# Half the key stores, and each head's 128 key rows as two loads of the same 64 rows

## The reference, cut to what matters

```python
x = _ln(src) * (1.0 + scale) + shift
q = (x @ Wq + bq).reshape(B, S, N_HEAD, HEAD_DIM).transpose(0, 2, 1, 3)
k = (x @ Wk + bk).reshape(B, S, N_HEAD, HEAD_DIM).transpose(0, 2, 1, 3)
v = (x @ Wv + bv).reshape(B, S, N_HEAD, HEAD_DIM).transpose(0, 2, 1, 3)
scores = jnp.einsum('bhqd,bhkd->bhqk', q / math.sqrt(HEAD_DIM), k)
scores = scores + attention_bias                     # 2 x 16 x 2048 x 2048 floats, 512 MB
scores = jnp.where(src_mask, -jnp.inf, scores.astype(jnp.float32))
probs = jax.nn.softmax(scores, axis=-1).astype(v.dtype)
ctx = jnp.einsum('bhqk,bhkd->bhqd', probs, v)
ctx = ctx.transpose(0, 2, 1, 3).reshape(B, S, D)
x = x + (ctx @ Wo + bo)
h = _ln(x) * g2 + beta2
ff = _gelu2(h @ W1 + b1) @ W2 + b2
return x + ff
```

## Time and profile before

| | |
|---|---|
| median of 3 runs | 3504.41 us (3502.69 to 3505.73) |
| the profiled execution's own time | 3502.99 us |
| its span, first to last instruction | 3501.3 us |
| mean granted TensorE clock | 0.992 |
| PE busy (matmul) | 3415.7 us, 98% |
| DVE, POOL, ScalarE busy | 2486.0 us (71%), 2084.9 us (60%), 1885.6 us (54%) |
| main memory read, written | 763.12 MB, 142.61 MB |

### The profile page before, as it was taken

The page is one execution under the profiler, slowest core; times in us unless marked ns, Lnnn a source line. Parts: engine busy times, 40 slices in busy tenths (PEclk is TensorE's granted clock), DMA queues, the critical chain, the costliest instruction groups (busy, mean ns, idle before and its releaser), DMA issues.

```text
span 3501.3 us, 60955 instructions
## 1 busy us (share of the span) xinstructions
PE 3415.7 (98%) x18338; PEld 1940.2 (55%) x18338; DVE 2486.0 (71%) x4176; ACT 1885.6 (54%) x2541; POOL 2084.9 (60%) x646
## 2 busy tenths in 40 slices
PE   8999799999999999999999999998899999999998
PEld 3444466666666666666666666665344444444443
DVE  5666599999999999999999999997434333343331
ACT  3222388888888888888888888886111111111110
POOL 0000499999899999999998999996202201211100
PEclk9999899999999999999999999999999999999999
DMA  8999999999999999999999999999402211210100
GB/s 290 340 338 339 360 365 349 344 348 351 399 344 348 350 350 345 394 352 349 351 343 367 378 351 347 346 351 324 107 19 54 72 32 40 72 51 21 48 12 12
DMA packets 288702, 906.20 MB, mean 259 GB/s; under 512 B 93344, under 2 KB 93344, under 8 KB 211360
## 3 DMA queue, kind: packets, MB, share of 16 engines
q1 hardware_dynamic: 240272, 811.43, 64.8%
q10 hardware_dynamic: 45840, 86.00, 7.0%
q0 software_dynamic: 2560, 8.39, 0.6%
HBM read 763.12 MB, written 142.61 MB: 259 GB/s over the span
## 4 chain that ended last, share of the span: by engine, by line
PE 86%; DVE 1%; DMA 1%; issue 0%; ACT 0%; SPq 0%; POOL 0%; DVEq 0%; ACTq 0%
PE b_T L765 27%; PE bank_ctx L788 14%; PE scores L731 14%; PE scores L1309 13%; PE b_T L1320 9%; PE bank_ctx L1320 3%; PE scores L1290 3%; PE scores L737 1%; DMA penb<-in_L_cond_b 1%; PE scores L1250 0%; PE scores L1299 0%; PE b_T L1326 0%; DVE probT L1151 0%; PE scores L1264 0%; ACT penb L1049 0%
## 5 line engine op out<-in xcount | busy, mean ns | idle before, releaser
L590 POOL TENSOR_TENSOR ring<-ring,penb 128x1856 f32<-128x1856 f32 x512 | 1904.5, 3759 | 502.1 <-DMA penb<-pen_scratch 416.8
L685 ACT ACTIVATE ring<-ring,low 128x2048 f32<-128x2048 f32 x512 | 1028.9, 2010 | 318.1 <-DVE low L654 318.1
L765 PEld LDWEIGHTS b_T<-ident,ring 128*128 128x128 f32 x8192 | 889.3, 141 | 434.2 <-DVE probT L638 430.8
L765 PE MATMUL b_T<-ident,ring 128*128 128x128 f32 x8192 | 1091.1, 276 | 6.5 <-DVE probT L638 5.9
L654 DVE CUSTOM_DVE_ANT_0 ring<-scores,ring 128x1024 f32<-128x1024 f32 x512 | 627.1, 1225 | 177.0 <-PE scores L731 153.8
L638 DVE COPY probT<-b_T 128x512 f32<-128x512 f32 x1024 | 702.0, 686 | 3.9 <-PE b_T L765 3.8
L654 DVE CUSTOM_DVE_ANT_0 ring<-scores,ring,low_part 128x1024 f32<-128x1024 f32 x512 | 652.6, 1275 | 0.4
L731 PE MATMUL scores<-keys,queries 128*128 (+1 forms) x2048 | 621.1, 424 | 21.1 <-DMA queries<-q_rows 16.7
L788 PE MATMUL bank_ctx<-probT,values 128*32 128x512 f32 x4096 | 546.2, 605 | 0.1
L695 ACT COPY probT<-b_T 128x512 f32<-128x512 f32 x1024 | 537.7, 575 | 0.2 <-PE b_T L765 0.2
L1016 POOL TENSOR_TENSOR keys_again<-keys_again,values 128x512 f32<-128x512 f32 x32 | 40.4, 1263 | 779.1 <-DVE values L1239 779.1
(11 more groups left out here) (131 smaller groups left out, 1930.9 us busy)
## 6 DMA issues: line engine op xcount, KB each, us to landing
ring<-in_fside_Bx16xSxS SPq DMA_DIRECT2D x512, 1024.0 KB, 7.4
keys<-k_rows SPq DMA_DIRECT2D x64, 1024.0 KB, 8.5
values<-v_heads ACTq DMA_DIRECT2D x128, 256.0 KB, 6.2
queries<-q_rows SPq DMA_DIRECT2D x128, 256.0 KB, 8.0
ctx_scratch<-ctxp ACTq DMA_DIRECT2D x128, 256.0 KB, 6.6
penb<-ctx_scratch SPq DMA_DIRECT2D x120, 256.0 KB, 4.7
k_rows<-part_hi SPq DMA_DIRECT2D x64, 256.0 KB, 3.3
k_rows<-part_lo SPq DMA_DIRECT2D x64, 256.0 KB, 3.4
```

Of the source, the lines that this page charges most:

```text
L590: nc.gpsimd.tensor_tensor(ring[:, j, 0:POOL_MASKED], ring[:, j, 0:POOL_MASKED], penb[:, j, 0:POOL_MASKED], ALU.add).then_inc(masked, 1)
L685: nc.scalar.activation(ring[:, k, :], ring[:, k, :], ACT.Exp, bias=low[:, k:k + 1], scale=-1.0, accum_out=column(sums_all, trip, k)).then_ ...
L765: last = nc.tensor.transpose(turn_bank(slot, n)[:, c * P:(c + 1) * P], ring[:, slot, at:at + P], ident[:])
```

## The change

`k_rows` keeps one high and one low part per head, 64 rows instead of 128. Its stores per block fall from four to two, and the load of a head's keys becomes two loads of the same 64 rows, one onto partitions 0 to 63 and one onto 64 to 127: the keys are then high, low, high, low. The queries' parts are reordered to high, low, low, high, so that the four products are the same. The counts of the semaphores follow.

```diff
-        STORES = 2 * 64 + 16
+        STORES = 32 + 64 + 16
...
-                        parts = (part_hi, part_lo, part_lo, part_hi) if g < DB else (part_hi, part_lo, part_hi, part_lo)
+                        parts = (part_hi, part_lo) if g < DB else (part_hi, part_lo, part_lo, part_hi)
...
-                    dve.wait_ge(stored[i], u * STORES + 64 * (g // 4) + 16)
+                    dve.wait_ge(stored[i], u * STORES + (0, 32, 96)[g // 4] + 16)
...
-                    sp.dma_start(keys[:, bass.ds(it % 2, 1), :].rearrange("p o n -> p (o n)").bitcast(F32),
-                                 of_head(k_rows, b, h)).then_inc(k_in, 16)
+                    for half in range(2):
+                        sp.dma_start(keys[half * 2 * DH:(half + 1) * 2 * DH, bass.ds(it % 2, 1), :].rearrange("p o n -> p (o n)").bitcast(F32),
+                                     of_head(k_rows, b, h)).then_inc(k_in, 16)
...
-                    pe.wait_ge(k_in, it * 16 + 16)
+                    pe.wait_ge(k_in, it * 32 + 32)
...
-    k_rows = nc.dram_tensor("k_rows", (B * DB, 4 * P, S), F32, kind="Internal").ap()
+    k_rows = nc.dram_tensor("k_rows", (B * DB, 2 * P, S), F32, kind="Internal").ap()
```

## The result

The changed kernel takes 3551.97 us in the median of 4 runs (3530.62 to 3567.51), against 3504.49 for the kernel before in the same comparison: +47.5 us, ratio 1.0132 [1.0078, 1.0186]. The forecast was 3510, in a range of 3502 to 3519. The time is outside it, and on the side to which 0.37 was given. Its runs also lie 37 us apart, where those of the kernel before lie within 3 us.

A forecast was written before the change was run, and what follows sets the result against it. The prediction took TensorE as the bound, with the DMA queue a close second that binds at the attention's start. Its terms, 2.5 + 1.25 + 1.7 = 5.5 us, gave 3508.5 for the profiled execution and 3510 for the median, range 3502 to 3519.

The forecast's parts named there:

- The stores: First stage: removing 64 stores, about 40 us of queue, gains 0, since TensorE's own work covers them.
- The seam: Between first stage and attention, 377 to 382 us: taken as 0, at most -4.5 us; rival of faster, chance 0.05.
- One more issue per head: SyncE issues one more DMA per head, 0.35 us, with the queries load 0.6 us later: costed at 0.
- the lead: Time from POOL's sum ending to DVE's starting: 6.98 us in steady state, 2.04, 1.37, 2.42 behind group starts, 0.13 at start.
- the half price: Key loads away from an empty queue: a pair of halves costs 1.25 us extra, half of the upper value 2.5.
- First head: Start of the attention: queries stand behind the keys in the queue, so +2.5 us.
- Second head: Second head of the attention: keys issued with DMA engines at 1.02 and a lead of 0.13 us, so +1.25 us.
- Group starts: Three later group starts: two key loads, 2.5 us, against leads of 2.04, 1.37 and 2.42, so +1.7 us in sum.
- two loads less the lead behind the start: Later group starts: two key loads at 1.25 us each, less each lead, leave 0.5, 1.1 and 0.1 us.
- Steady state: Attention's other heads: the lead of 6.98 us covers even 2.5 and the queue has 5.4 us room per head, so 0.
- The rival of a bound queue: Steady state: at DMA share 0.96 only 1.3 us per head is free, so +77 us, 3580; chance 0.07.
- The rival that the halves cost 2.5 us each wherever the queue is backed up: Start 5.0 and group starts 9.2 us, together +14.2, 3519; chance 0.24.

The follow-up runs named there:

- one copy: Kernel before with whole key loads, plus behind each a 1 MB copy from main memory to main memory that nothing waits for but the end: 3523.56 us, ratio 1.0055.
- Loads alone: Kernels without the layer that only load side rows onto different sets of partitions: one MB by two halves takes 4.8 us and not 2.5.
- the light queue: Kernel before with all stores and keys in halves, one of eight side tiles not loaded outside the groups' first heads: 3531.66 us, ratio 1.007.
- the two doses: Kernel before with whole key loads and one or two unwaited 1 MB memory copies behind each: 3523.56 us with one, 3565.24 us with two.

## Why the prediction was wrong

**What held.** The stores are worth nothing, with TensorE's work as their cover. The seam is 5.15 us in both. One more issue per head is nothing in the time of the whole (3505.39). The start and the group starts are where the queue's time goes into the end, and the lead is what covers it elsewhere. The queue has more room in the steady state than its share of 0.96 says: one copy fitted in. The key loads' median landing is 1.5 us longer, as expected.

**The steps that failed: the price of a pair, and a path that was left out.** The forecast had both ends of it from the earlier trace rows, none and 2.5 us, and took 2.5 for the first head alone and 1.25, "the half of it", everywhere else, because one half might fill while some engines were at the other. Loads alone show no such overlap: 4.8 us for each MB by halves in a row, where 1.25 extra would be 3.75. So the half price was wrong: a pair costs 2.2 us extra or more in every list of loads. And the upper end was not an upper end: 2.6 and 3.3 were measured between whole loads, and 3.3 to 4.2 is the estimate in the kernel. By term:

- First head: +2.5. The change's profile has 5.64 behind the seam. The halves with all stores, the light queue and the halves in first heads only have 2.2, 2.2 and 2.1, near the forecast. But one profile's figure is good to some 1.5 us only: two loads by columns, at full width, have 1.6 and 1.0 there, and those on every second partition -0.3. The query load was also issued 1.0 us later in those three and 1.5 in the change, where 0.6 was forecast and costed at nothing. How much of the 2.2 is width isn't told apart.
- Second head: +1.25. Heads 1 and 2 took 4.8 us more. A copy of 2.5 us takes 2.8 there, so here the whole price counts and the lead of 0.13 us covers none of it. In the change TensorE waits 3.75 us of them for the queries.
- Group starts: 0.5 + 1.1 + 0.1. They took 9.0, 11.1 and 6.2. Two sizes were off. The price is one: 2 x 4.2, by the estimate above, and not 2 x 1.25. The rule "two loads less the lead behind the start" is the other. At a price of 2.5 it gives 3.0, 3.6 and 2.6, and the copies, which cost just that, took 4.2, 4.2 and 4.1: it is 1.1 us short in the mean. It knows only the path through POOL. The path of the query load, which it had at nothing behind the first head, shows at each of these starts: TensorE waits for it 2.1 us each with a copy, 4.6, 0.6 and 3.5 with the change, and the clock falls there. Where it doesn't show, with one pair per group, the rule holds: 1.5, 1.3 and 0.5. With 4.2 and 1.1 more the rule gives 22.7 in sum, where 26.3 were measured.
- Steady state: 0. Here it was +13 in this execution. The cover was worked out for at most 2.5 us, and for 2.5 it holds: one copy fits without loss. The rival of a bound queue had 0.07 and said that it decides from 1.3 us per head on, which is wrong, since that copy is 2.5. With the pairs the queue runs at a share of 1.00, the least lead of a head is 0.1 to 5.8 us where the forecast's lead was 6.98, and where it is near 0 a late tile goes into the end. With 2.5 us taken out of the queue this part was gone.

The rival that the halves cost 2.5 us each wherever the queue is backed up gave 3519. With that price paid, by the copy, the kernel takes 3523.6. So it had the right mechanism, and its sum over the places was 5 us short. The remaining 28 us are put down to a price above 2.5; that is argued from the two doses and the loads alone, and no run shows such a price paid in the kernel without halves. How much of it is the clock isn't told apart either.

**What stays open.** Why a pair costs the queue more between wide transfers than the sum of its halves, why the change's first head was 3.4 us slower than the same step in the other kernels with halves (its query load went out only 0.5 us later than theirs), and whether loading the same 64 rows twice costs something on top of the halves (15 us between medians, intervals overlapping; neither the loads alone nor the kernel with every second partition shows any). The spread of 37 us between runs goes with it: it isn't there with copies (4 us for one, 8 for two), nor with whole loads.

**No version beats both kernels.** The change with its rows on every second partition is as fast as the kernel before and stores 16.8 MB less. Here that is worth nothing.

## What to carry to other kernels

Look at which partitions a transfer reaches, not only at its bytes: a load onto one half of them costs twice its time in the queue and more, and splitting it over both halves in turn gives nothing back, while the same bytes onto every second partition run at nearly the full rate, 393 of 424 GB/s in a row and without loss between whole loads. Follow every load that stands behind the changed one to who waits for it: a lead on one path says nothing of another. Where a queue is nearly full, don't price a change by its share of busy time: put in a copy of known size that no one waits for, and read from it how much room there is and what a microsecond of queue costs at each start. And when the bounds of an unlisted price come from a clean sum, leave room above it, for what stands behind the transfer in a shared queue.

## What the runs showed that was not expected

- Two transfers onto every second partition run at 393 GB/s, two onto the lower and upper half at 219 to 220, with the same bytes in the same number of transfers.
- Halves issued by two engines at once, SyncE the lower and ScalarE the upper, reach 240 GB/s only.
- The effect reaches what stands behind the pair. In the attention, from 500 to 2300 us, one in ten of the 2 KB packets on SyncE's queue, which are the queries', takes 173 ns or more (84 before). Its 8 KB packets have a 90th percentile of 589 ns (374 before), but the halves' own packets are 11% of them, so that figure is mostly the halves themselves.
- The queue carries 423 to 424 GB/s of whole loads with no pause, and 412 in the kernel with two copies a head, so that 349 at a share of 0.96 was not near its end.
